# The first spreads of q and k one head at a time, GpSimd copying the middle parts and starting on the weights later

## The reference

```python
qkv = (einsum('bnd,ed->bne', x, qkv_w) + qkv_b).reshape(b, n, 16, 24)
q, k, v = split(qkv, 3, axis=-1)
attn = softmax(einsum('bhqd,bhkd->bhqk', q, k) * 8 ** -0.5)
out = einsum('bhqk,bhkd->bhqd', attn, v)
a = einsum('bnd,ed->bne', out, fc_w) + fc_b + x
x = layernorm(x + a)
h = silu(tlin(x, w1)) * tlin(x, w2)
h = gelu(tlin(h, h1)); h = gelu(tlin(h, h2))
x = layernorm(x + tlin(h, w3))
```

## Time and profile before

| | us |
|---|---|
| median of 3 runs (lowest, highest) | 323.77 (323.39, 324.91) |
| profiled execution, device time | 322.21 |
| its span, first to last instruction | 320.4 |
| TensorE busy in the span | 295.8 (92%) |
| VectorE busy | 244.1 (76%) |
| ACT busy | 234.8 (73%) |
| GpSimd busy | 148.8 (46%) |
| mean granted TensorE clock | 0.965 of full |

### The profile page before, as it was taken

The page is one execution under the profiler, slowest core; times in us unless marked ns, Lnnn a source line. Parts: engine busy times, 40 slices in busy tenths (PEclk is TensorE's granted clock), DMA queues, the critical chain, the costliest instruction groups (busy, mean ns, idle before and its releaser), DMA issues.

```text
span 320.4 us, 5569 instructions
## 1 busy us (share of the span) xinstructions
PE 295.8 (92%) x1804; PEld 138.5 (43%) x1804; DVE 244.1 (76%) x516; ACT 234.8 (73%) x433; POOL 148.8 (46%) x227
## 2 busy tenths in 40 slices
PE   8567998999997999999999999999999999999991
PEld 6421132422332344334544233625634353579990
DVE  3959899998989899998996859298684410289883
ACT  3562567999683896898688998697799989447340
POOL 6762038651043793118807778063478913610201
PEclk9985899999999899999999999999999999999996
DMA  5643353313211321212030023310100010000101
GB/s 151 184 92 54 58 192 88 55 24 51 35 19 18 68 36 16 42 22 43 0 57 29 6 47 48 71 20 0 33 4 2 2 33 0 4 0 2 33 2 38
DMA packets 17830, 13.44 MB, mean 42 GB/s; under 512 B 2551, under 2 KB 16648, under 8 KB 17800
## 3 DMA queue, kind: packets, MB, share of 16 engines
q1 hardware_dynamic: 17546, 12.85, 19.2%
q10 hardware_dynamic: 254, 0.20, 0.2%
HBM read 5.51 MB, written 1.05 MB: 20 GB/s over the span
## 4 chain that ended last, share of the span: by engine, by line
PE 60%; ACT 11%; DVE 9%; POOL 8%; issue 6%; DMA 4%; SPq 1%; ACTq 1%; POOLq 0%; DVEq 0%
PE bank L445 26%; PE bank L480 11%; PE bank L465 9%; PE bank L456 6%; DVE negmax L803 6%; ACT prob L654 4%; DMA h_nat<-in_L_ffn_h_w_dram 3%; PE bank L420 2%; ACT L654 2%; POOL hT L990 2%; POOL parts L960 2%; PE bank L531 1%; ACT h_nat L729 1%; PE bank L438 1%; PE bank L503 1%
## 5 line engine op out<-in xcount | busy, mean ns | idle before, releaser
L803 DVE TENSOR_REDUCE negmax<-bank 128x1 f32<-128x512 f32 x256 | 160.2, 682 | 23.0 <-PE bank L456 22.5
L654 ACT ACTIVATE prob<-bank 128x512 f32<-128x512 f32 x256 | 136.7, 604 | 29.0 <-PE bank L465 27.4
L480 PE MATMUL bank<-prob,v_sb 128*32 128x512 f32 x512 | 73.0, 608 | 0.4 <-ACT prob L654 0.3
L456 PE MATMUL bank<-stack 61*128 61x512 bf16 x256 | 65.9, 398 | 4.3 <-DMA stack<-parts 2.6
L445 PE MATMUL bank<-act,hT 128*128 128x512 f32 (+1 forms) x320 | 68.3, 359 | 0.1
L465 PE MATMUL bank<-stack 64*128 64x512 bf16 x256 | 61.4, 389 | 2.2 <-DVE negmax L803 1.0
L445 PEld LDWEIGHTS bank<-act,hT 128*128 128x128 f32 x320 | 49.2, 190 | 14.3 <-issue 6.4
L722 ACT ACTIVATE h_nat<-bank,hs_all 128x512 f32<-128x512 f32 (+1 forms) x40 | 22.8, 603 | 22.4 <-PE bank L445 22.4
L456 PEld LDWEIGHTS bank<-stack 61*128 61x128 bf16 x256 | 17.6, 94 | 49.7 <-issue 26.9
L978 POOL CAST mparts<-negmax 128x16 bf16<-128x16 f32 (+1 forms) x17 | 3.7, 219 | 74.3 <-DVE negmax L803 74.3
L465 PEld LDWEIGHTS bank<-stack 64*128 64x128 bf16 x256 | 14.0, 94 | 51.0 <-issue 36.2
(11 more groups left out here) (120 smaller groups left out, 343.0 us busy)
## 6 DMA issues: line engine op xcount, KB each, us to landing
stack<-parts SPq DMA_DIRECT2D x124, 48.0 KB
x_in<-in_L_attn_x_dram SPq DMA_DIRECT2D x4, 256.0 KB, 4.7
h_nat<-in_L_ffn_h_w_dram SPq DMA_DIRECT2D x1, 1024.0 KB, 8.1
work<-in_L_ffn_h_w_dram SPq DMA_DIRECT2D x1, 1024.0 KB, 5.6
res<-in_L_attn_x_dram SPq DMA_DIRECT2D x4, 256.0 KB, 2.9
out_dram<-y SPq DMA_DIRECT2D x3, 256.0 KB, 2.3
work<-in_L_ffn_w_w_dram SPq DMA_DIRECT2D x2, 256.0 KB, 3.0
stack<-mT SPq DMA_DIRECT2D x30, 6.0 KB
```

The lines of the kernel that those rows point to most:

```text
L456: nc.tensor.matmul(space("S", n)[:, :], stack[0][half_of(h, MROW), h // 2, qt * P:(qt + 1) * P], stack[1][half_of(h, MROW), h // 2, :], st ...
L480: last = nc.tensor.matmul(space("P", pfirst)[at:at + VW, :], v_sb[b % 2][:, kt, of:of + VW], prob[:, t % NP, :], start=kt == 0 and slot % ...
L654: nc.scalar.activation(prob[:, n % NP, :], space("T", n)[:, :], ACT.Exp, scale=SCALE).then_inc(emptied("T", n), 1)
L803: nc.vector.tensor_reduce(negmax[:, g % 2, col:col + 1], space("S", n)[:, :], AX.X, ALU.max, negate=True).then_inc(emptied("S", n), 1)
```

## The change

- `first_spread` takes one head per step. The list of k heads is dealt out by `ZK_ON_ACT` (heads 0 and 2) and `ZK_ON_SP` (the fourteen others); SP has 16 steps zq and 14 steps zk, ACT two steps zk with one head each instead of two with two.
- SP's order of the first spreads becomes two of q, six of k, eight of q, six of k, then the maxima's DMA of the second group, two of k and the last six of q. Before, it was eight heads of q, twelve of k, two of q, that DMA, and six of q.
- On ACT both steps zk stand behind the second da and ahead of x of the second batch, and of all evacuations of weights but the first.
- The copies of the middle part (db) of batch 0 go from VectorE to GpSimd, whose first db steps stand ahead of the weights. GpSimd's first wc also waits for lo of k.
- GpSimd's first m stands behind five wc and wl pairs instead of six.
- All five orders are new beyond the head too. They have the same steps in the same number, apart from the spreads, from db (VectorE 2 to 0, GpSimd 6 to 8) and from K (16 to 10). A step Z is defined for TensorE and is not in its order.

The code and the head of each order (the rest of the strings is left out):

```diff
-SP:   lw lh xin vb zq*4 zk*6 zq mrow zq*3 lh l3 xin mrow more xres xin spread
+SP:   lw lh xin vb zq*2 zk*6 zq*8 zk*6 mrow zk*2 zq*6 lh mrow l3 more xres xin spread
-PE:   x:0 wq:1 q:2 q:3 v:4 wt:5 wt:6 wt:0 wt:1 wt:2 wt:3 x:5 wf:6 v:0 S:5 S:4 S:6
+PE:   x:0 wq:1 q:2 q:3 v:4 wf:5 wt:6 wt:0 wt:1 wt:2 wt:3 wt:6 x:5 v:4 S:5 S:0 S:1
-ACT:  x q*2 da wt da wt*2 x zk wt zk wt wm wt wm*5 m mrow e
+ACT:  x q*2 da wt da zk*2 x wt wm wt*3 wm wt wm*3 m mrow wm e
-DVE:  wq r mid r lo mid db lo db v wf v s*41
+DVE:  wq r mid r lo mid lo wf v*2 s*43
-POOL: vz*2 wc wl wc wl wc wl wc wl wc*2 wl*2 m*3
+POOL: vz*2 db*2 wc wl wc wl wc wl wc wl wc wl m wc wl m*2
...
     LAST = B - 1
     HP = NK * NK
     TAIL_HP = 2 * (NK - 1) + NK
-    ACT_ZK = 2
+    ZK_ON_ACT = [0, 2]
+    ZK_ON_SP = [h for h in range(H) if h not in ZK_ON_ACT]
     ACT_M = 1
     GROUPS = [(0, 0, 2), (0, 2, 2)] + [(b, GH * j, GH) for b in range(B) for j in range(NG) if b or j]
     UNITS = [(b, 0, NT) for b in range(LAST)] + [(LAST, t0, 2) for t0 in (0, 2)]
@@ -338,16 +339,15 @@
 
             return (rep0[h], 32) if b == 0 else (rep[h // GH], 16 * 2 * GH * b)
 
-        def first_spread(eng, i, p):
-
-            if p % 2 == 0:
-                eng.wait_ge((zeros, ones)[i], p // 2 + 1)
-            if p == 0 or (i == 1 and p == ACT_ZK):
+        def first_spread(eng, i, heads, n):
+
+            h, at = heads[n], HD * head_of(heads[n])
+            if n == 0 or heads[n - 1] // GH < h // GH:
+                eng.wait_ge((zeros, ones)[i], h // GH + 1)
+            if n == 0:
                 eng.wait_ge((lo_q, lo_k)[i], 1)
                 eng.wait_ge((dup_q, dup_k)[i], 2)
-            for h in (2 * p, 2 * p + 1):
-                at = HD * head_of(h)
-                eng.dma_start(stack[i][half_of(h, SR), h // 2, :], parts[i][at:at + HD, :, :]).then_inc(rep0[h], 16)
+            eng.dma_start(stack[i][half_of(h, SR), h // 2, :], parts[i][at:at + HD, :, :]).then_inc(rep0[h], 16)
 
         block = ctx.enter_context(nc.Block())
 
@@ -367,9 +367,9 @@
                     sp.wait_ge(ps_xT, b)
                     sp.dma_start(x_in[:, :, :], x[b].rearrange("(t p) c -> p t c", p=P)).then_inc(ld_x, 16)
                 elif what == "zq":
-                    first_spread(sp, 0, n)
+                    first_spread(sp, 0, range(H), n)
                 elif what == "zk":
-                    first_spread(sp, 1, n + ACT_ZK)
+                    first_spread(sp, 1, ZK_ON_SP, n)
                 elif what == "spread":
                     b, j = 1 + n // NG, n % NG
                     sp.wait_ge(qk_lo, 2 * b)
@@ -612,6 +612,9 @@
                 elif what == "K":
                     until_free(pe, "K", n)
                     keep_busy(4, space("K", n)).then_inc(emptied("K", n), 1)
+                elif what == "Z":
+                    until_free(pe, "Z", n)
+                    keep_busy(2, space("Z", n)).then_inc(emptied("Z", n), 1)
                 elif what == "L":
                     pe.wait_ge(lo_max, 1)
                     until_free(pe, "L", 0)
@@ -683,7 +686,7 @@
                 elif what in ("ws", "wg"):
                     nc.scalar.activation(warm[:, :], ident[:, 0:1], (ACT.Silu, ACT.Gelu)[what == "wg"])
                 elif what == "zk":
-                    first_spread(act, 1, n)
+                    first_spread(act, 1, ZK_ON_ACT, n)
                 elif what == "mrow":
                     _, s0, ns = GROUPS[n]
                     until_empty(act, "m", n)
@@ -829,9 +832,6 @@
                                                        vb[:, :].rearrange("p (i j k d) -> p i j k d", j=PO, k=3, d=HD)[:, :, j, 2, :].unsqueeze(1).broadcast_to(
                                                            [P, NT, H // PO, HD]), ALU.add)
                     last.then_inc(emptied("v", n), 1)
-                elif what == "db":
-                    dve.wait_ge(qk_mid, n + 1)
-                    nc.vector.tensor_copy(parts[n][:, 4, :], parts[n][:, (3, 1)[n], :]).then_inc((dup_q, dup_k)[n], 1)
                 elif what == "or":
                     dve.wait_ge(ps_oT, n + 1)
                     if n:
@@ -959,10 +959,9 @@
                     for a in ((1, 2), (3, 5))[i]:
                         nc.gpsimd.tensor_copy(parts[i][:, a, :], parts[i][:, 0, :])
                 elif what == "db":
-                    n += 2
                     i = n % 2
                     pool.wait_ge(qk_mid, n + 1)
-                    nc.gpsimd.tensor_copy(parts[i][:, 4, :], parts[i][:, (3, 1)[i], :]).then_inc(qk_dup, 1)
+                    nc.gpsimd.tensor_copy(parts[i][:, 4, :], parts[i][:, (3, 1)[i], :]).then_inc((dup_q, dup_k)[i] if n < 2 else qk_dup, 1)
                 elif what == "mid":
                     n += 2
                     i = n % 2
@@ -984,6 +983,8 @@
                     nc.gpsimd.tensor_tensor(lo, left, mid, ALU.subtract).then_inc(m_parts, 1)
                 elif what == "wc":
                     until_empty(pool, "wt", n)
+                    if n == 0:
+                        pool.wait_ge(lo_k, 1)
                     nc.gpsimd.tensor_copy(wt_dst(n, 0), w_raw[n % len(w_raw)]).then_inc(hi_wt, 1)
                 elif what == "wl":
                     pool.wait_ge(hi_wt, n + 1)
```

Two places of TensorE's order that the prediction counts in, before and after. The first unit's f, X and A:

```diff
-f:6 q:4 q:5 T:2 T:3 T:1 S:6 S:0 P:7 T:4 T:2 S:6 S:3 P T:1 T:0 S:4 S:2 P S:6 S:1 m:3 x:0 P S:5 X:4 S:3 S:0 S:2 T:6 T:1 A:4 B:6
+f:5 S:1 S:3 P S:0 S:6 m:2 q:5 q:4 x:2 S:1 S:3 P S:0 S:2 T:5 T:6 T:4 X:5 T:6 T:1 T:4 T:6 P T:1 T:3 T:4 S:5 S:6 A:0 B:1
```

The end of the last attention step and the tail:

```diff
-P T:2 P*2 K:0*5 T:0 P T:6 K:1*2 P K:0*2 o:5 K:0*2 a:4 a:3 K:0 f:1 H:2 H*3 H:0 H*3 f:6 H:7 H*3 H:5 H*3 X:4 K:0 X:3 W:1 W A:2
+P*4 T:6 T:5 T:4 T:0 P T:1 K:2*2 P K:0*2 o:3 K:0 H:2 a:6 a:5 H*2 f:4 H H:0 H*3 H:1 H*2 f:7 H H:3 H*3 X:6 K:0 W:5 W A:4 X:2
```

More of the change, by code:

```diff
@@ L8 @@
 SP_ORDER = """
-lw lh xin vb zq*4 zk*6 zq mrow zq*3 lh l3 xin mrow more xres xin spread mrow spread mrow spread mrow spread mrow spread xres mrow spread mrow spread
-mrow spread mrow*2 spread xres mrow spread mrow spread out spread mrow xres mrow*2 out*4
+lw lh xin vb zq*2 zk*6 zq*8 zk*6 mrow zk*2 zq*6 lh mrow l3 more xres xin spread mrow spread xin mrow spread mrow spread mrow xres spread mrow spread
+mrow spread mrow spread mrow xres mrow spread*2 mrow spread out mrow spread mrow*2 xres mrow out*4
@@ L18 @@
[L18 to L21, removed]
@@ L42 @@
+w3 e*6 u e*5 m e*2 o e*8 h e*2 h*2 e*3 h e g e m e*12 o e*3 m e*2 h e*3 h e*3 a e h e h g m e*9 t e t u t*2 e w3 e*4 u*2 e*2 u e*3 o e m e*12 h e*3 h
+e h e*3 h g e*8 wg o a*2 h*4 ws t*8 w3 wg h*15 w3 h w3
 """
 DVE_ORDER = """
-wq r mid r lo mid db lo db v wf v s*41 r s r lo s*2 lo s hs s*19 or s om s*6 wx s*4 L s*19 v s or s om s*4 l1 s l1 r s l1 s lo s l1 s r s l1 lo s*2 Xh
-s Xl s*4 t s*6 t s*4 t s*4 t s*3 or s om s*42 v or om r*2 s*3 lo l1 lo l1 s l1 s l1 s*3 l1 s*2 Xh s Xl s*5 t*2 s t s*2 t s*15 or om s*3 l2 s l2 s l2 s
@@ L47 @@
-l2 s*4 l2 s*14 or s om s*6 l1 s l1 s l1 s l1 s l1 s*3 Xh s Xl s*5 t s*4 t s t*2 l2*4 or om l2 or om l1*5 gh gl l1 gh l1 gl l1*2 gh gl l1 Xh gh Xl gl
-Xh Xl gt*2 h0 gt l0 gt h0 gt l0 h0 gt l0 h0 gt l0 gt h0 l0 h0 l2 l0 l2 h0 l2 l0 l2 h0 gh l0 gl gh l2 gl gh gl gh*2 gl gh gl gh gl gh gl gh gl gh gl gh
-gl gh gl*2 gh gl gh gl gh*2 gl l2 gl l2*9
+wq r mid r lo mid lo wf v*2 s*43 r s r s lo s lo s*2 hs s*13 or s om s*6 wx s*2 L s*23 v or s om s*8 l1 s l1 s l1 s l1 s r s r l1 s lo Xh s Xl s lo
+s*3 t*4 s*12 or om s*37 v or s om s*3 l1*3 s l1 s*3 l1 s*2 Xh s Xl s*3 r s r s*4 lo s t s t s*3 t*2 s lo s*5 l2*4 s*6 or s om s l2 s*34 or s om s*4
@@ L50 @@
+l1*2 s l1 s l1 s*3 l1 s*3 Xh s Xl s*3 t*3 s t s*2 l2 s l2 s l2*2 or om l2 or om l1*4 gh gl l1 gh gl l1*3 gh l1 gl Xh Xl l1 gh gl Xh gt Xl gt h0 gt l0
+gt h0 gt l0 gt h0 gt l0 gt h0 l2 h0 l0 h0 l0 h0 l0 h0 l0 gh l0 gl gh l2 gl gh l2 gl gh l2 gl gh gl gh l2 gl gh*2 gl gh gl gh gl gh gl gh gl*2 gh gl gh
+gl gh gl l2 gh l2 gl l2*8
 """
 POOL_ORDER = """
-vz*2 wc wl wc wl wc wl wc wl wc*2 wl*2 m*3 da mid da db mid db xr m wc wl wc wl wc wl wc wl m wc wl m*2 da*2 mid db p1 mid db m u h0 l0 xr u h0 l0 u
@@ L54 @@
-h0 l0 u m h0 l0 m*2 gh gl gh gl gh*2 gl*2 mid*2 da m da db*2 p1 xr u*2 m u*2 gh gl gh gl gh gl gh gl m h0*3 l0*3 h0 l0 p2 m gh*2 gl*2 gh gl gh gl m p1
-xr gh gl gh gl gh gl gh gl m u*2 h0 l0 u*2 h0 l0 h0 l0 h0 l0 p2 gh gl gh gl gh gl gh gl p1*2 p2*3
+vz*2 db*2 wc wl wc wl wc wl wc wl wc wl m wc wl m*2 da*2 mid db mid db xr m wc wl wc wl wc wl wc wl wc wl m*3 da p1 da mid db mid db xr m u*2 h0 l0
+u*2 h0 l0 h0 l0 h0 l0 m*2 gh*4 gl*4 m p1 xr gh da m da gl mid gh gl gh gl gh gl db u mid db h0 l0 u h0 l0 m u h0 l0 u h0 l0 p2 m gh*4 gl*4 m*2 p1 gh
```

45 lines of the change are left out of this document (24 added, 21 removed).

## The result

The changed kernel takes **328.93 us** (328.24 to 329.88) against 323.58 us for the kernel before on the same chip: ratio 1.0147, 95% interval 1.0076 to 1.0219. That is 1.5% slower, outside the predicted range; the quotient of the two medians, 1.0165, is a little higher and lies in the interval. The profiled execution took 329.88 us, its span is 328.1 us.

What follows compares the result with a forecast made beforehand. VectorE's row maxima were taken to bound the head, TensorE the rest. Gains of 0.7 us in the head and 0.6 us in the tail made 1.3 us, so the median 323.77 became 322.5 us; range 320.0 to 325.8 us.

Steps and rivals of the forecast that it cites:

- Part 1: Head: copies on GpSimd let spreads start at 10.25, S follow v at 17.26, and maxima come 2.0 us earlier.
- Part 2: Head: GpSimd's weight pairs hold the first m to 24.4, leaving 0.7 us gain at the first T and P.
- Part 3: New orders beyond the head: most of the middle set at 0, three places examined, 0.6 us gained in the tail.
- (a): Third batch's x load, issued later on SP: lands at 50.6 with 1.7 us slack, so costs nothing.
- rival C: Third batch's x lands late and TensorE waits: slower, 325.9 us at the 8.4 us landing; chance 0.12.
- (b): First unit: later f makes TensorE wait some 2 us at X; X and A together 0, bounds -1.5 to +1.5.
- (c): Tail: three H ahead of the last-but-one f in place of K gain 0.6 us net.
- D: Head: GpSimd's subtractions take 1.6 us instead of 1.26, so the earlier start brings nothing: 323.8 us; chance 0.20.
- B: Head: clock is full at the first P, which comes near 31.3; with the tail 3.3 us gained, 320.5 us; chance 0.22.
- 0.15 for slower: Chance of over 325.4 us: 0.11 from rival C, 0.04 where (b) goes to its bound and D holds too.

Runs made afterwards that it cites:

- e15: Changed head with its first 21 S on re-laid banks, old order behind it, plus seven K in the weight-load wait: 322.30 us, ratio 0.9972 to before.
- e6: Changed kernel with the fourth m of TensorE and ACT placed three S and three e later: 330.24 us, ratio 1.0160 to before.
- e9: Changed order on all engines up to the first unit's X, old order behind it with banks renamed: 329.16 us, ratio 1.0135 to before.
- e11: Changed order on all engines up to the 241st T, old order behind it: 328.90 us, ratio 1.0134 to before.
- e14: Kernel before with seven K added in the wait for the weight load: 324.13 us, ratio 1.0014 to before.
- e8: Changed kernel with ACT's last gelu of the batch loop behind three of the exponentials that followed it: 330.80 us, ratio 1.0219 to before.
- e2: Old head, up to the first T, in front of the changed order of everything behind it: 332.48 us, ratio 1.0235 to before.
- e10: Old order on all engines up to the first unit's X, changed order from there: 329.27 us, ratio 1.0141 to before.
- e12: Old order on all engines up to the 241st T, changed tail behind it: 324.57 us, ratio 0.9980 to before.
- e3: Changed kernel with 14 K added in the wait for the weight load: 330.37 us, ratio 1.0159 to before.
- e13: Changed kernel with seven K added in the wait for the weight load: 329.11 us, ratio 1.0166 to before.
- e17: Changed kernel with seven K in the load wait, two small matmuls behind each 5th to 14th S, K ahead of first m and T: 329.68 us, 1.0185 to before.

## Why the prediction was wrong

- **Part 1, spreads and first S.** The spreads were right (10.64 for 10.25, no S waits). The first S was wrong in the profiled execution: 20.72 instead of 17.3. The failed term is v's end, which I took over from before with its transposes at full clock. At half clock they, x and v cost 1.71 + 0.46 + 0.91 = 3.1 us more, and the load came 0.5 us later. Where the clock was full the rest of the step holds: first S 17.29 in e15 and 17.48 to 17.66 in e6, e9 and e11, without any fill; the 17th maximum 2.03 us earlier than before in e15 (2.0 predicted).
- **Part 2, GpSimd's weights and P.** Right in mechanism: m starts straight behind a weight subtraction, in after at 26.80, in e15 at 24.29 (24.4 predicted), first T 29.53 (29.4), first P 32.09 (32.1 to 32.3); in e6, e9 and e11 it is 31.70 to 31.95. Whether the 0.7 us lasts to the end stays open: against before's profile none of it is left in e15, against e14's 0.76 us. My sum had no term for when the clock comes back, and that varies by more than 0.7 us: 1.6 us (e8) to 4.7 us (e2) behind the first P.
- **Part 3, "most of the middle I set at 0".** This is the step that made the prediction wrong: the term was put at nothing, and it measured 5.6 us in after's profile and 5.4 in e2's, from the 17th exponential to the last H. Both orders being dense says nothing on 0.7 us here and there: the new one loses 1.9 us more from 40 to 99, 0.4 to 2.0 from 99 to 114, as the clock has it, and 2.4 from 180 to 264, in waits of 0.7 to 1.7 us for GpSimd's m (57.95), the layernorm (104.39), GpSimd's act (190.29), an exponential (213.10) and a maximum (240.97), in the order of the rows above. I looked at three places of some 300 us and gave the remainder no bound.
- **(a)** Right: x of the third batch was there, and rival C false; at 54.80 it waits for a bank.
- **(b)** The wait at X was predicted as some 2 us and is 1.71. That nine more steps would give it back was wrong: behind the wait the clock was at half from 104.76 to 111.58 us (3.4 us of that before, from 103.40), where P takes 1.93 us instead of 1.06, and the stretch costs 2.0 us more, past my bound of 1.5. In e2 and e10, with the same order there and 3.4 us at half clock, it costs 0.6 us more, within the bound: the wait was foreseen, the clock behind it had no term. The Trainium skill, "TensorE: Matmul & The Clock Gate", section "HAM oscillation", has waits between bursts bring back the half clock; by these rows it does at X too, and I had applied it to the head only.
- **(c)** The 0.6 us in the tail didn't come out of it. By its times e12 leaves it open: 0.9980 is 0.6 us less, with an interval of 1.3 us either way, and the medians are 0.1 us apart. The profiles say what happened. The H taken ahead do pay: from the last P to the last H the shift falls by 0.95 us in after, e3, e6, e13 and e17 (by 0.16 to 0.4 where the half clock lasted 6.8 us). But as much is lost just ahead: from the 241st T to the last P it grows by 0.95 us in after, by 1.7 in e12. What I counted at nothing there was the K that went. My text has the five K behind the last softmax work; they stand ahead of the last two T, where the old order fills the waiting for ACT's last exponentials with them for 2.22 us. The new one has no K there and waits 2.81 us. The waiting is about the same, but behind the empty one the clock was at half in each of the ten profiles that have the new tail, and in none of the old.
- **Rivals.** D's longer subtractions didn't come (1.26 us each in after and e15); its outcome for the head, nothing, can't be told from the forecast's 0.7 us by these runs. B's full clock at the first P came in no profile, e17 with its fills included (its first P takes 1.92 us). My 0.15 for slower hung on single mechanisms (C, or b with D), none of which is the one that came. The mistake was to give a new order from end to end no rival of its own.

## What to carry to other kernels

Where a change comes with a new written order for all engines, that order can be the larger part of the change, as here: give it a term and a bound of its own, even if the edit that it came with is small. Join the two orders at a step where the counts agree, first behind the edit: that says within one run which part carries the difference, where moving single steps says only that others wait in their place. Where the clock's levels differ from one execution to the next, one pair of profiles can't tell a gain under 1 us: set it beside several executions of each kernel, or beside profiles in which the clock came back at the same step.
